# Two transformer layers on one core: low parts of four w1 tiles stored 64 bytes off in each feed-forward

## What is computed

```python
# layer 0
h = film(rmsnorm(x, norm2_w), cond, film2_w, film2_b)
h = jax.nn.gelu(h @ mlp_w1 + mlp_b1, approximate=False) @ mlp_w2 + mlp_b2
return x_in + h
...
# layer 1
x_mod2 = _modulate(_ln(x), shift_mlp, scale_mlp)
h = jax.nn.gelu(x_mod2 @ w_mlp1 + b_mlp1)
mlp_x = h @ w_mlp2 + b_mlp2
x = x + gate_mlp[:, None] * mlp_x
```

## The kernel before

| operand | role | modulo 256 |
|---|---|---|
| w1 high and low, B and D | weights of up | 128 |
| g_hi, g_lo, B and D | weights of down | 128 |
| m_h_hi, m_h_lo | moving in up | 64 |
| w2 high and low, B and D | moving in down | 64 |
| A_m_hi, A_m_lo, A_v_hi | stage A | 128 |
| a_h_hi, a_h_lo | stage A | 64 |
| A_vp_hi, A_vp_lo | stage A, moving | 0 |
| C_wt_proj (moving) and C_y_hi, C_y_lo (weights) | stage C | 128 and 192 |

## Time and profile before

### The profile page before, as it was taken

The page is one execution under the profiler, slowest core; times in us unless marked ns, Lnnn a source line. Parts: engine busy times, 40 slices in busy tenths (PEclk is TensorE's granted clock), DMA queues, the critical chain, the costliest instruction groups (busy, mean ns, idle before and its releaser), DMA issues.

```text
span 1594.8 us, 42633 instructions
## 1 busy us (share of the span) xinstructions
PE 1560.0 (98%) x14314; PEld 1399.4 (88%) x14314; DVE 1307.9 (82%) x2953; ACT 846.7 (53%) x1696; POOL 483.1 (30%) x639
## 2 busy tenths in 40 slices
PE   8999999999999999999999999999997999999999
PEld 7999998999999998677777777777775999999999
DVE  5798888787777777788888888888885888888886
ACT  3566664343333343667777767776666333333333
POOL 2333322131111223243433434433333322222221
PEclk9999999999999999999999999999999999999999
DMA  5600002111111112333333333333331232222222
GB/s 175 216 21 20 20 20 72 66 43 52 40 53 39 53 41 65 107 107 98 108 106 106 112 96 106 105 102 111 100 104 63 80 100 92 94 90 94 89 94 68
DMA packets 147362, 132.72 MB, mean 83 GB/s; under 512 B 23552, under 2 KB 129984, under 8 KB 147280
## 3 DMA queue, kind: packets, MB, share of 16 engines
q1 hardware_dynamic: 147120, 131.61, 25.9%
q0 software_dynamic: 160, 0.04, 0.1%
HBM read 54.61 MB, written 24.54 MB: 50 GB/s over the span
## 4 chain that ended last, share of the span: by engine, by line
PE 89%; DVE 6%; issue 2%; DMA 1%; ACT 1%; SPq 0%; DVEq 0%; ACTq 0%; POOL 0%; POOLq 0%
PE bank L209 61%; PE bank L1733 8%; PE bank L1715 7%; PE bank L1677 5%; PE bank L1743 2%; PE bank L393 2%; DVE D_g_hi L1084 1%; PE bank L1751 1%; PE bank L765 1%; PE bank L465 1%; DVE D_g_lo L1086 1%; PE bank L191 1%; ACT D_g L1076 0%; PE bank L556 0%; DMA A_w_film<-in_L_cond_film_w 0%
## 5 line engine op out<-in xcount | busy, mean ns | idle before, releaser
L1824 ACT ACTIVATE C_probs<-bank 128x1024 f32<-128x1024 f32 x256 | 262.7, 1026 | 157.6 <-PE bank L1715 157.2
L1689 DVE TENSOR_REDUCE C_negmax<-bank 128x4 f32<-128x1024 f32 x248 | 303.4, 1223 | 48.5 <-PE bank L1677 44.6
L1076 ACT ACTIVATE D_g<-bank,D_bias 128x256 f32<-128x256 f32 x256 | 107.5, 472 | 223.0 <-PE bank L209 212.3
L1076 ACT ACTIVATE B_g<-bank,B_bias 128x256 f32<-128x256 f32 x256 | 107.5, 471 | 222.2 <-PE bank L209 222.2
L358 POOL TENSOR_TENSOR m_small<-m_small,consts 128x2 f32<-128x2 f32 x64 | 48.9, 763 | 476.9 <-DVE m_small L349 239.4
L209 PE MATMUL bank<-D_wt_w_hi,D_g_lo 128*128 128x256 f32 x512 | 144.7, 283 | 3.8 <-DVE D_g_lo L1086 3.4
L209 PE MATMUL bank<-B_wt_w_hi,B_g_lo 128*128 128x256 f32 x512 | 144.8, 283 | 3.2 <-DVE B_g_lo L1086 3.0
L1715 PEld LDWEIGHTS bank<-C_qs,C_kx 64*128 64x128 f32 x1024 | 77.3, 185 | 78.7 <-ACT C_probs L1824 46.0
L209 PE MATMUL bank<-m_h_hi,B_wt_w_lo 128*128 128x256 f32 x512 | 143.6, 281 | 0.0
L209 PE MATMUL bank<-B_wt_w_lo,B_g_hi 128*128 128x256 f32 x512 | 143.4, 280 | 0.0
L209 PE MATMUL bank<-B_wt_w_hi,B_g_hi 128*128 128x256 f32 x512 | 143.4, 280 | 0.0
(11 more groups left out here) (263 smaller groups left out, 4931.4 us busy)
## 6 DMA issues: line engine op xcount, KB each, us to landing
C_qs<-C_q_hi SPq DMA_DIRECT2D x128, 128.0 KB
C_kx<-C_k_hi SPq DMA_DIRECT2D x128, 128.0 KB, 2.6
C_qs<-C_q_lo SPq DMA_DIRECT2D x64, 128.0 KB
C_kx<-C_k_lo SPq DMA_DIRECT2D x64, 128.0 KB, 2.1
C_gbc<-mod_rows SPq DMA_DIRECT2D x32, 256.0 KB, 3.4
D_gbc<-mod_rows SPq DMA_DIRECT2D x32, 256.0 KB, 3.4
turned<-N_blocks SPq DMA_DIRECT2D x31, 256.0 KB, 2.0
N_back<-turned SPq DMA_DIRECT2D x124, 64.0 KB, 2.0
```

The costliest lines, as they stand in the source:

```text
L1076: ins = eng.activation(o, p, func, bias=per_seq(bias1, 2 * u + d, b))
L1689: e_max.by(eng.tensor_reduce(m4[:, :, :, j], spair[:, :].rearrange("p (e q k) -> p e q k", e=2, q=TH), AX, ALU.max, negate=True))
L1824: e_exp.by(eng.activation(probs[t % NP][:, :], stpair[:, :], ACT.Exp, scale=scl))
```

## The change

The low part of w1 gets another layout in both feed-forwards. Tiles 0, 2, 4 and 6, the first weights of the four up groups, are stored together at the start ("lead"), then come 16 unused elements (64 bytes), then the other twelve tiles. `part` finds a tile's place; `emit_lo` writes lead and rest with an instruction each, so the two parts that hold both kinds (elements 0 to 511 and 512 to 1023) need two instructions of 2x128 elements. The base of the low part moves by 64 bytes, so that the rest stays at 128 modulo 256 and the lead is at 64. At the steps from a down group to an up group, 61 x 2 of them in each feed-forward, the address difference is then 0 modulo 256 (256 modulo 512). All other steps within B and D keep 64, and the order of TensorE's instructions is the same.

To make room without moving the rest, `consts` goes (its four columns live in unused columns of the two small tiles), layer 1's bcol goes into the temporary region, its low part is placed ahead of the high part, gap2 goes, and gap_m grows. Where TensorE comes from stage A or C into a first up product, the difference changes as well, at one or two places each (0 becomes 192 or so modulo 256).

```diff
+LEAD, LEAD_GAP = (0, 2, 4, 6), 16
...
-            def __init__(self, sb, sem, name, view):
+            def __init__(self, sb, sem, name, view, lead=(), lo_first=False):
                 self.view, self.t, self.N = view, view.shape[0] // P, view.shape[1]
+                tiles = range(self.t * self.N // P)
+                self.lead, self.rest = list(lead), [i for i in tiles if i not in lead]
+                self.rest_at = len(lead) * P + (LEAD_GAP if lead else 0)
+                self.lo_first = lo_first
...
             def place(self, sb):
-                self.hi = sb("wt_" + self.name + "_hi", [P, self.t * self.N], F32R)
-                self.lo = sb("wt_" + self.name + "_lo", [P, self.t * self.N], F32R)
+                n = self.t * self.N
+                if self.lo_first:
+                    self.lo = sb("wt_" + self.name + "_lo", [P, n + self.rest_at - len(self.lead) * P], F32R)
+                self.hi = sb("wt_" + self.name + "_hi", [P, n], F32R)
+                if not self.lo_first:
+                    self.lo = sb("wt_" + self.name + "_lo", [P, n + self.rest_at - len(self.lead) * P], F32R)
...
-                eng.tensor_tensor(self.lo[:, c], self.raw[:, c], self.hi[:, c].bitcast(F32), ALU.subtract).then_inc(self.s_lo, 1)
+                if not self.lead:
+                    eng.tensor_tensor(self.lo[:, c], self.raw[:, c], self.hi[:, c].bitcast(F32), ALU.subtract).then_inc(self.s_lo, 1)
+                    return
+                raw, hi = (t[:, :].rearrange("p (i c) -> p i c", c=P) for t in (self.raw, self.hi))
+                for start, group in ((0, self.lead), (self.rest_at, self.rest)):
+                    mine = [i for i in group if part * n <= i * P < (part + 1) * n]
+                    if not mine:
+                        continue
+                    step = mine[1] - mine[0] if len(mine) > 1 else 1
+                    src = slice(mine[0], mine[-1] + 1, step)
+                    o = start + group.index(mine[0]) * P
+                    ins = eng.tensor_tensor(self.lo[:, o:o + len(mine) * P].rearrange("p (i c) -> p i c", c=P),
+                                            raw[:, src], hi[:, src].bitcast(F32), ALU.subtract)
+                ins.then_inc(self.s_lo, 1)
...
             def part(self, k, c0, n):
-                return self.hi[:, k * self.N + c0:k * self.N + c0 + n], self.lo[:, k * self.N + c0:k * self.N + c0 + n]
+                c = k * self.N + c0
+                o = c
+                if self.lead:
+                    assert n == P
+                    i = c // P
+                    o = self.lead.index(i) * P if i in self.lead else self.rest_at + self.rest.index(i) * P
+                return self.hi[:, c:c + n], self.lo[:, o:o + n]
...
-        scale1m, consts = sb("scale1m", [P, KT * NB]), sb("consts", [P, 8])
-        neghalf, one_rows, zero_col = consts[:, 0:TH], consts[:, TH:TH + 1], consts[:, TH + 1:TH + 2]
+        scale1m = sb("scale1m", [P, KT * NB])
+        neghalf, one_rows, zero_col = small["a_"][:, 22:24], small["m_"][:, 22:23], small["m_"][:, 23:24]
...
-                sb("gap_m", [P, 8])
+                sb("gap_m", [P, 16])
...
-                self.bcol = sb("bcol", [P, HT])
                 if not layer:
+                    self.bcol = sb("bcol", [P, HT])
                     sb("gap1", [P, 16])
-                self.w = [Weight(sb, sem, "w1", a[n1])]
+                self.w = [Weight(sb, sem, "w1", a[n1], LEAD, layer == 1)]
...
-                sb_tmp("next_rest", [P, 448])
+                sb_tmp("next_rest", [P, 448 - HT])
+                mlp.bcol = sb_tmp("next_bcol", [P, HT])
...
-            sb_near("gap2", [P, 16])
```

## The result

| | before | after |
|---|---|---|
| timed executions, median | 1588.16 us (1587.48 to 1600.56, 4) | 1604.34 us (1602.89 to 1605.68, 4) |
| profiled execution | 1596.58 us | 1605.68 us |
| its span | 1594.8 us | 1603.9 us |
| granted TensorE clock, mean | 0.995 | 0.990 |

The ratio of after to before is 1.0079, 95% interval 1.0045 to 1.0113. The change makes the kernel slower by 0.8% (between the two medians it is 1.0%). The median lies 8 us above the forecast of 1596.3 and outside its range, near what rival 3 priced (1602).

The account below looks back on a forecast made before the run. TensorE's matmul pace was taken as the bound, busy 1560.0 of 1594.8 us. Terms -3.5 + 1.9 + 0.9 + 0 + 0.3 + 0.1 = -0.3 us took the profiled 1596.58 to 1596.3; own range 1594 to 1599, 8-in-10 range 1587 to 1599.5.

Parts of the forecast that it names:

- rival 3: Changed steps leave TensorE long; D's two stretches cost 4.7 us, short parts some 1 us: 1602; chance 0.10.
- B's great stretch: Stage B, 348.4 to 585.4 us: 2014 long steps go from 117.8 to 116.0 ns, 3.5 us less.
- The rest of B: The other 1,058 matmuls of stage B, both paces with waits between: +0.3 us, bounds -1.8 and +2.9.
- D's first stretch: Stage D, 1252.0 to 1332.9 us: 716 short steps go from 113.3 to 116.0 ns, 1.9 us more.
- D's end: Stage D, 1554 to 1591 us: 328 steps, each 2.7 ns slower, 0.9 us more.
- D's loop: Stage D's hardware loop, 1333 to 1554 us: pace hidden by waits on VectorE, 0 us; upper end 1.0 more.
- The split subtractions: Low parts of w1's first half, two 256-wide subtractions instead of one 512-wide, beside TensorE's stream: +0.1 us.
- The cover: Stage B: VectorE waited 51.0 us for gelu, so has room for a TensorE 1.5% faster; without it -3.5 becomes 0.
- The coin: Waits pick TensorE's pace anew, spreading timed runs from 1587.6 to 1601.3 us; the change makes every run average, 1596.3.
- Rival 1: The changed step does nothing, since its difference is 256 modulo 512: 1588.5 median, 1587 to 1601 a run; chance 0.12.
- Rival 2: The changed step always leaves TensorE short; B's stretch saves 9.0 us, rest of B up to 1: 1587; chance 0.09.
- Rival 4: The flips come, but the profiled execution is slower than timed ones by a fixed 8 us: 1588.3; chance 0.15.

Follow-up runs that it names:

- the one at 192: Changed kernel with the lead moved so each down-to-up step has difference 192 modulo 256: 1583.74 us median, ratio 0.9948 to the kernel before.
- the two kernels with both stages locked at 0: The changed kernel, 1604.34 us, and the same with its lead 320 instead of 64 bytes off (difference 0 modulo 512), 1604.36 us.
- the first three experiments: TensorE-alone map of odd steps; changed kernel without its 16-element gap, 1596.41 us; changed kernel with difference 0 modulo 512, 1604.36 us.
- the kernels of TensorE alone: Newly written kernels without the reference's computation, only 128x256 matmuls with new weights at varied address differences; 113.3, 117.8 or 120.0 ns a step.
- the first map: TensorE alone: blocks of 24 matmuls at difference 320, odd steps between them at 0 to 992 bytes; blocks took 2.72 or 2.83 us.

## Why the prediction was wrong

**What bounds the kernel.** Right. The changed kernel and the one at 192 differ by 20.6 us at the median (taken at different times, but 0.8% above and 0.5% below the kernel before give the same) and 22.7 between the profiled executions, with the same instructions but for two bias copies in two pieces each. 12.5 + 6.4 of the 22.7 lie in B and D by their up products, 2.7 between them.

**The step that failed** is the sentence "So a difference of 0 does not choose a pace. It flips it." Each step in the earlier trace rows on which it rested was the pair (0,64): the weights 0 from the moving operand ahead, but 64 from their own (A_m_lo at 128 with a_h_hi at 64, a_h_lo at 64 with A_vp_hi at 0, D_wt_w_lo at 128 with m_h_hi at 64). That step exchanges the paces 8 of 8 times. The change moved w1's lead to 64, which put it at 0 also to its own m_h_hi. That pair, (0,0), leaves long 8 of 8 times. The prediction had named one difference where there are two, and the table of addresses held the second. That this second difference decides is shown; why TensorE behaves so is not.

**The terms.**

- B's great stretch, -3.5: measured 0 (2015 records before and after). It stayed long and nothing was gained.
- The rest of B, +0.3: the whole of B gave +2.9, all of it here. That it equals the upper bound given is luck, since the bound was 1,058 steps x 2.7. Of B's steps some 600 were short before and some 120 are after, so some 480 x 4.5 = 2.2 us; the other 0.7 was not taken apart.
- D's first stretch, +1.9: 716 steps x (117.8 - 113.3) = 3.2. D's end, +0.9: 328 x 4.5 = 1.5. Both bare, as said.
- D's loop, 0 with bounds 0 and +1.0: 5.6 - 3.2 - 1.5 = 0.9, at the upper end. The pace was hidden by the waits only in part. In 1345 to 1545 us this kernel has 1677 records, the one at 192 has 1701, and the kernel before had

```profile
1345.00:1545.00 200.00, 198.11 (x1684) 195.14 (x1683) 170.40 (x368) 73.16 (x176) 47.59 (x53) 1.00 0.28 92
```

so a sequence (96 matmuls) takes 11.45 us in this kernel, 11.29 in the one at 192 and 11.40 before: nearly all short against nearly all long gains 0.16 us of the 0.43 that 96 x 4.5 ns would be.

- The split subtractions, +0.1. Hidden, as said, as far as the runs can tell: the kernel with them and without the difference is no slower than before. On VectorE a half took 0.414 us where the whole took 0.679, so two halves are 0.15 us more each time, 0.3 in all:

```profile
L203 DVE TENSOR_TENSOR B_wt_w_lo<-B_raw_w,B_wt_w_hi x4: 414/414/416, 80.6 to 88.6; 128x256 fp32r<-128x256 f32 x4
```

**The cover** for a quicker B was real. VectorE's wait for gelu in all of B is 75.9 us before and 79.0 after, and the kernel at 192 ran B at the short pace for 12 us less.

**The timed runs.** The coin fits what was measured: the spread is 13 us before and again 13 us with difference 64 in the new layout, but 2.8 and 2.1 us in the two kernels with both stages locked at 0. That each run would be nearly the same held; the value did not, since a lock replaces a coin by one of its faces, and this was the long one. It is not a fair coin, and not all: beside the first three experiments the kernel before took 1595.98 us or more in all of 15 executions, one of them 1606.46, above the 1601.3 that the prediction's two paces allow.

**The rivals.** Rival 3 came true by its mechanism and its place ("the first up group of B keeps 118 ns after a short group"). Its price, 1596.6 + 4.7 + 1 = 1602.3 for a profiled execution, was 3.4 us under the 1605.68 measured: it gave the short parts of B and of D's loop together 1 us where B gained 2.9 and D's loop 0.9, and 0.6 lies outside B and D. Rival 1 fell with the 23 steps entered short and left long. Rival 2's 1587 is what the difference of 192 gives (1583.74 measured), not this one. Rival 4 fell: the timed runs lie 0.9 to 2.8 us below the profiled one, not 8.

The Trainium skill ("SBUF — State Buffer", Who interferes with whom) says that TensorE never waits on anyone, with independent read ports for its two operands. No run here tests that against other engines, but its two operands are not independent of each other: in the kernels of TensorE alone the same matmul starts 113.3, 117.8 or 120.0 ns after the one before, by address. The skill's rule of N/2.4 + 2.5 ns ("TensorE: Matmul & The Clock Gate", Back-to-back issue gap) is given there for a matmul by itself, and gives an estimate of 109 ns here; with new weights each time it was reached at no difference that was tried.

## What to carry to other kernels

Where back-to-back matmuls with new weights each run at two paces, list for each odd step the address of its weights against both moving operands, the one ahead and its own, before saying what it does: a rule read from traces holds only for the pairs in them. A spread of timed runs that is wider than an experiment's effect is itself a lead, here a pace that can change at a wait and that the next hundreds of matmuls keep. Look for a step that locks the better one: here a difference of 192 in place of 0 at one step in 24 is worth 20.6 us, and 0.5% against the kernel before.

## What the runs showed of the hardware

- A 128x256 float32r matmul with new weights each time runs at 113.3 or 117.8 ns at a granted clock of 1.00 where the difference is 64 or 192 modulo 256, and keeps its pace: 2015 records in a row long (all at 64), 1847 short (at 64, with every 24th at 192). At a difference of 0 at every step it takes 120.0 ns.
- A single step with another difference sets, keeps or exchanges the pace of the matmuls behind it, in blocks of 24 and in B's stretches of hundreds. In the first map the pattern repeats every 256 bytes. The weights' address counts against the moving operand ahead and against their own.
- The long pace has more than one state inside: (128,128) gave short from one and long from another. What lies behind the two paces is not shown by any run.
